# Four-layer graph network on one core: layer 1's aggregations run over four PSUM banks, and the out-attention's steps stand at other places

## The reference, cut to what matters

```python
def _gat_heads(x, adj, W, a):
    Wh = einsum('bnf,hfo->bhno', x, W)
    f1 = einsum('bhno,ho->bhn', Wh, a[:, :O])
    f2 = einsum('bhno,ho->bhn', Wh, a[:, O:])
    e = f1[:, :, :, None] + f2[:, :, None, :]
    e = where(e > 0, e, 0.01 * e)
    e = where(adj[None, None] > 0, e, -1e9)
    return einsum('bhnm,bhmo->bhno', softmax(e, axis=-1), Wh)
h = elu(_gat_heads(x, adj, W_heads, a_heads))
h = transpose(h, (0, 2, 1, 3)).reshape(B, N, -1)
out = elu(_gat_heads(h, adj, W_out[None], a_out[None])[:, 0])
y = maximum(out @ w1 + b1, 0) @ w2 + b2 + out
```

## Time and profile before

| | |
|---|---|
| timed runs | median 3086.3 us of 3 (3083.88 to 3086.51) |
| profiled execution | 3088.17 us, its span 3086.5 us |
| layer 0 | to about 417 us of the span |
| layer 1, the loop over pairs | first `project` at 425.8 us, last `out_part` before 2156 us |
| PE busy | 3025.1 us (98% of the span) |
| DVE, POOL, ACT busy | 75%, 69%, 56% |

### The profile page before, as it was taken

One profiled execution on the slowest core, in us unless ns is written; L12 is line 12 of the kernel. 1 busy time (PEld: TensorE's weight loads), 2 busy tenths in 40 slices (PEclk: granted clock), 3 DMA queues, 4 the chain that ended last, 5 costly groups with the idle time before them and its releaser, 6 DMA issues.

```text
span 3086.5 us, 65234 instructions
## 1 busy us (share of the span) xinstructions
PE 3025.1 (98%) x19324; PEld 2655.5 (86%) x19324; DVE 2321.6 (75%) x4877; ACT 1726.6 (56%) x4250; POOL 2120.1 (69%) x2901
## 2 busy tenths in 40 slices
PE   8999989999999999999999999999799999999997
PEld 7888878888998988888889888898688888888885
DVE  7777646777777777777777777675788888888885
ACT  3333335555555555555555555553577677776675
POOL 5666645666676666667666666651588888888885
PEclk9999989999999999999999999999999999999999
DMA  5555421112111111211111111112623333233220
GB/s 201 181 187 177 154 83 32 52 44 54 38 54 48 51 51 44 54 38 54 48 48 54 44 50 42 54 45 71 189 90 102 93 101 94 89 99 102 92 75 32
DMA packets 308643, 247.65 MB, mean 80 GB/s; under 512 B 150060, under 2 KB 215644, under 8 KB 308316
## 3 DMA queue, kind: packets, MB, share of 16 engines
q1 hardware_dynamic: 296796, 221.64, 24.1%
q10 hardware_dynamic: 9216, 16.78, 1.4%
q0 software_dynamic: 2560, 8.39, 0.8%
HBM read 162.83 MB, written 83.91 MB: 80 GB/s over the span
## 4 chain that ended last, share of the span: by engine, by line
PE 79%; issue 3%; POOL 3%; DVE 1%; DMA 0%; ACT 0%; SPq 0%; POOLq 0%; DVEq 0%; ACTq 0%
PE hp L2048 24%; PE wop L2062 23%; PE wop L47 9%; PE hp L2188 5%; PE hp L47 5%; PE agg L2031 5%; PE shared L2070 2%; PE shared L2155 2%; PE agg L2155 2%; PE shared L262 1%; POOL g_terms L1361 1%; POOL cols L403 0%; PE smallp L212 0%; PE smallp L101 0%; POOL x1b L1374 0%
## 5 line engine op out<-in xcount | busy, mean ns | idle before, releaser
L1293 POOL TENSOR_TENSOR w_first<-xd,v_row 128x512 f32<-128x512 f32 x480 | 690.9, 1452 | 351.1 <-DMA xd<-x_scratch 275.8
L2048 PE MATMUL hp<-yT_hi,big_hi 128*128 128x256 f32 x2048 | 583.7, 285 | 1.4 <-DVE yT_lo L1737 1.4
L2048 PE MATMUL hp<-yT_hi,big_lo 128*128 128x256 f32 x2048 | 580.7, 284 | 0.0
L2048 PE MATMUL hp<-yT_lo,big_hi 128*128 128x256 f32 x2048 | 580.4, 283 | 0.0
L2062 PE MATMUL wop<-big_hi,hT_hi 128*128 128x512 f32 x1024 | 424.7, 415 | 0.0
L1754 DVE TENSOR_TENSOR hT_lo<-ex,hT_hi 128x512 fp32r<-128x512 f32 x256 | 258.6, 1010 | 200.9 <-ACT hT_hi L1452 198.3
L2062 PE MATMUL wop<-big_hi,hT_lo 128*128 128x512 f32 x1024 | 401.5, 392 | 0.0
L2062 PE MATMUL wop<-big_lo,hT_hi 128*128 128x512 f32 x1024 | 400.0, 391 | 0.0
L2048 PEld LDWEIGHTS hp<-yT_hi,big_hi 128*128 128x128 f32 x2048 | 393.5, 192 | 6.8 <-DVE yT_lo L1737 1.7
L2048 PEld LDWEIGHTS hp<-yT_lo,big_hi 128*128 128x128 f32 x2048 | 393.6, 192 | 1.2
L2048 PEld LDWEIGHTS hp<-yT_hi,big_lo 128*128 128x128 f32 x2048 | 393.6, 192 | 0.0
(11 more groups left out here) (215 smaller groups left out, 8009.2 us busy)
## 6 DMA issues: line engine op xcount, KB each, us to landing
x0f<-in_x_turned SPq DMA_DIRECT2D x64, 256.0 KB, 2.7
xt<-in_x SPq DMA_DIRECT2D x64, 256.0 KB, 3.0
x_scratch<-w_first ACTq DMA_DIRECT2D x64, 256.0 KB, 2.3
xa<-x_scratch SPq DMA_DIRECT2D x64, 256.0 KB, 2.7
att_hi_scratch<-att_hi SPq DMA_DIRECT2D x64, 256.0 KB, 2.0
att_lo_scratch<-who SPq DMA_DIRECT2D x64, 256.0 KB, 2.0
att_hi<-att_hi_scratch SPq DMA_DIRECT2D x64, 256.0 KB, 3.6
att_lo<-att_lo_scratch SPq DMA_DIRECT2D x64, 256.0 KB, 4.3
```

The costliest lines, as they stand in the source:

```text
L1293: nc.gpsimd.tensor_tensor(terms[:, k % TR, :], xd[:], v_row[:, k, :], ALU.mult).then_inc(terms_ready, 1)
L2048: ins = nc.tensor.matmul(hp[half][:, s * 2 * P:(s + 1) * 2 * P], a, b, start=c == 0 and i == 0, stop=c == KC - 1 and i == 2)
```

## The change

It turns `smallp` and `shared` into one tensor `agg_b` of two banks that is the second target of `aggregate`. Tile 0 of a pair goes to `agg`, tile 1 to `agg_b`, in one call for both. The four halves are carried off in the order of `EVICTED`. What uses `smallp` and `shared` in between stands behind `banks_free`, which waits until all four are off. `at.dve_before_exp` is split in two calls for every second tile. The lists of all five engines are written anew; DVE's, ACT's and POOL's instructions are the same in number and shape.

```diff
     def dve_before_exp(self, nc, dve, t, p, j, fill):
+        self.dve_add(nc, dve, t, p, j)
+        self.dve_peak(nc, dve, t, fill)
...
-            smallp = pb("smallp", [P, D])
-            shared = pb("shared", [P, D])
+            agg_b = pb("agg_b", [P, 2, D])
+            shared, smallp = agg_b[:, 0, :], agg_b[:, 1, :]
+            banks = (agg, agg_b)
+            EVICTED = ((0, 0), (1, 0), (0, 1), (1, 1))
...
-                def y_hi(p, q, j, side):
+                def y_hi(p, q, n):
+                    j, side = EVICTED[n]
                     act.wait_ge(agg_done, 4 * p + 2 * q + j + 1)
                     ge(act, h_done, 2 * (4 * p + 2 * q + side - 1))
-                    ge(act, y_lo_ready, 2 * (4 * p + 2 * q + j) + side)
+                    if n > 1:
+                        act.wait_ge(y_lo_ready, 4 * (2 * p + q) + n - 1)
...
-                def aggregate(p, q, j):
+                def aggregate(p, q, before):
+                    a = 2 * p + q
+                    for j in range(2):
+                        pe.wait_ge(at.turned_ready, 2 * (2 * p + j + 1))
+                        pe.wait_ge(xa_loaded[j], 16 * p + 16)
+                        ge(pe, y_lo_ready, 4 * a - 1 + j)
+                        if j == 1:
+                            before()
+                        for c in range(KC):
+                            for g in range(2):
+                                own = slice(g * NODES, (g + 1) * NODES)
+                                ins = nc.tensor.matmul(by_head(banks[j][:, g, :])[:, :, c, :],
+                                                       xa[j][own, c * P:(c + 1) * P],
+                                                       at.turned[own, j, 2 * q:2 * q + 2, :], start=True, stop=True)
+                        ins.then_inc(agg_done, 1)
+                def banks_free(p, q):
+                    pe.wait_ge(y_lo_ready, 4 * (2 * p + q) + 4)
```

More of the change, by code:

```diff
@@ L1335, in step @@
                     if fresh(p + 2):
[L1336 to L1342, removed]
+                        products_of(*second, range(0, 2))
                     if pair(m):
@@ L1494, in step @@
-                    if pair(p + 1):
-                        if later(p):
-                            dots(*d1, (2,))
+                    if fresh(p + 2):
+                        dots(*first, (0,))
                     if pair(p - 2):
                         split_att(2 * (p - 2) + 1, 1, p - 1)
[L1499 to L1504, removed]
+                    exp(k, 1)
@@ L1521, in step @@
+                    for n in range(3):
+                        y_hi(p, 1, n)
+                    if pair(p + 1):
+                        at.act_exp(nc, act, 2 * p + 3)
+                    y_hi(p, 1, 3)
+                    h_hi(k + 1, 0)
+                    if fresh(p + 2):
+                        dots(*first, (5, 6))
+                    h_hi(k + 1, 1)
                     if pair(p + 1):
                         at.act_turned(nc, act, 2 * p + 2, p + 1, 0, agg_done)
-                    if pair(p):
-                        exp(k + 1, 1)
@@ L1829, in step @@
                     if pair(m):
                         ao_.dve_after_exp(nc, dve, 2 * m)
-                    if pair(p + 1):
-                        at.dve_before_exp(nc, dve, 2 * p + 3, p + 1, 1, fill1)
-                    if pair(p):
-                        elu(k + 2, 0)
+                    for n in range(4):
+                        y_lo(p, 1, n)
+                    h_lo(k + 1, 0)
+                    if pair(m):
+                        out_f(2 * m + 1, 1)
                     if pair(p + 1):
@@ L1855, in step @@
-                    if pair(p):
-                        elu(k + 3, 1)
-                    if pair(p + 1):
-                        y_lo(p + 1, 0, 1, 0)
-                    if pair(p):
-                        h_lo(k + 3, 0)
-                    if pair(p + 1):
-                        y_lo(p + 1, 0, 1, 1)
-                for j in range(2):
-                    for side in range(2):
-                        y_lo(0, 0, j, side)
+                        for n in range(4):
+                            y_lo(p + 1, 0, n)
@@ L1867, in _ @@
+                    h_lo(k + 3, 0)
+                for n in range(4):
+                    y_lo(0, 0, n)
                 dve.wait_ge(a_loaded, 16)
@@ L2118, in step @@
                         ao_.pe_scores(nc, pe, 2 * m + 1, same_graph)
-                    if pair(p):
-                        out_part(p, 1, 3)
-                    if pair(m):
-                        pe.wait_ge(at.turned_ready, capped(2 * (2 * p + 4), 2 * T))
-                        out_sums(2 * m, 0)
-                    if pair(p + 1):
-                        aggregate(p + 1, 0, 0)
-                    if pair(p):
-                        project(p, 3)
+                    for c in range(KC):
+                        out_part(p, 1, c)
```

343 lines of the change are left out of this document (141 added, 202 removed).

## The result

The changed kernel is slower: median 3174.26 us of 4 runs (3173.82 to 3176.88), against 3085.89 us of 4 runs of the kernel before. The ratio is 1.0289, interval 1.0271 to 1.0307. The prediction said 3075.0 with a range of 3053 to 3100, so the result lies outside it, on the side of the rivals. The profiled execution took 3176.88 us, its span 3175.2 us.

What follows compares the result with a forecast made beforehand. It took TensorE's blocks to bound the kernel at 54.17 us a step; -1.02 saved, +0.8 wait and -0.1 gaps gave 53.85, in all -11.3 us, so 3075.0 us, range 3053 to 3100.

Steps and rivals of the forecast that it cites:

- What bounds the kernel: Layer 1 steps: TensorE's blocks alone set the step, 54.17 us, apart from short issue gaps of 0.34 us.
- first rival: TensorE in layer 1's steps: no wait at all, 3051 us; chance 20%.
- Part 2: Small transpositions and scores on TensorE: placing them side by side saves about 0.08 per pairing, 0.24 us a step.
- Part 1: TensorE's aggregations: two runs of 32 passes replace four of 16, saving 0.39 us twice, 0.78 a step.
- the gaps called issue: TensorE's short gaps, mostly ahead of transpositions: 0.34 us a step, expected to shrink by 0.1.
- Part 3: TensorE at banks_free(p, 1), ahead of at's transposition: a new wait of 0.8 us a step for the last y_lo.
- the other new waits come out with room: TensorE's waits at both transpositions of ao, banks_free(p + 1, 0) and att_ready: room of 0.8 to 2 us, no cost.
- the second one: VectorE held up behind GpSimd's products, making the banks_free wait 1.5 us a step: 3096 us; chance 20%.
- The third: A second new wait behind out_part(p, 1), for ao's probabilities and att_ready: 3105 us; chance 8%.
- That the run saves nothing: Aggregation over four banks: nothing saved, 0.78 us a step dearer, 3100 us; chance 7%.
- The prediction's own sign of being wrong: TensorE's waits fall on another block, or the part outside layer 1 changes by more than 2 us.
- the case without a wait: TensorE in layer 1's steps never waits at the new places: 3051 us; chance 20%.

Runs made afterwards that it cites:

- e9: Changed kernel with ao's add first, two out_part chunks ahead of the run, who's copy earlier, product 5 later, dot 5 behind an exp: 3051.75 us.
- e10: As e9, but the two out_part chunks stand between the tiles of aggregate(p, 1), splitting one run: 3063.82 us.
- e7: Changed kernel with GpSimd's product 5 of the first tile moved behind the out-attention's probabilities: 3118.21 us.
- e2: Changed kernel with two of the four chunks of out_part(p, 0) moved ahead of aggregate(p, 1), the run left whole: 3093.04 us.
- e8: Changed kernel with three moves: ao's add first, two out_part chunks ahead of the run, who's copy ahead of dots 1 and 2: 3081.16 us.
- e1: Changed kernel with the first operation (add) of the out-attention's softmax moved ahead of at.dve_peak in VectorE's list: 3089.41 us.
- e6: Changed kernel with two out_part chunks placed between the tiles of aggregate(p, 1), so that run is split in two: 3095.18 us.
- e4: Changed kernel with the copy of who, keep_wo(m, 0), moved ahead of dots 1 and 2 in ScalarE's list: 3157.31 us.

## Why the prediction was wrong

**What bounds the kernel** was right for the kernel before, and the sum of TensorE's blocks was priced well: without a wait the prediction gave 3051 for its first rival, and e9 has 3051.75. That it is so near is luck in part, since two of its terms were off in opposite ways (Part 2).

**Part 1** held. One run of 32 passes is 1.98 us. e10 shows that it saves 0.34 us beside a score, and the blocks put it at 0.40 without one; I had taken 0.39.

**Part 2** was wrong where it was tried. The transposition costs 0.11 at either place, so its switch to float32 and back was never the price I had made of it. The pairing of the score with out_sums was not tried alone, but the chain of e9 shows the same 0.17 with and without it. So the 0.24 a step was nothing. In its place came two gains that I had put lower or not at all. A step was 54.17 in the mean and 53.96 without the gaps called issue, so these gave 0.21 and not 0.1; and an out_part in one piece takes 5.47 us where two halves took 2.75 each, 0.03 for each of the three that are no longer cut.

**Part 3** is where it failed. The two times that it counted came out: `who` was put at T + 13.2 and came at T + 13.4 (out_f starts at 13.7), the last `y_lo` at T + 25.8 and came at T + 26.0. The second is luck in part: `h_lo` and the first elu together took 1.4 us more than their terms, held up by GpSimd, and `at.dve_peak` with ao's own operations 1.2 us less. But both times were held against one wait alone, `banks_free(p, 1)`. The step "the other new waits come out with room" listed four others and left out the one inside the run, `scores_read`, although the diff shows it as an argument of `aggregate`; so this wait stood in the sum at nothing, with no reason given. The prediction's own terms give it a price: 13.2 + 2.3 for out_f and natural + 0.98 for h_lo + 1.3 for the one elu that stands there + 2.45 for `at.dve_peak` + 0.2 for L109 itself put the end of the read at T + 20.4; TensorE, with 5.75 + 5.5 + 0.24 + 5.75 + 0.17 + 1.09, is there at T + 18.5. That is a wait of about 2.0, and behind it `banks_free` costs nothing. The step would have been 54.17 - 1.02 + 2.0 - 0.1 = 55.05, and the forecast, with the prediction's other small terms, near 3111: slower, which is the right way, and still too low. The measured wait is 2.93, which by the same sum gives 3139; it is longer because `who` and out_f came 0.45 later and `h_lo` and the elu took 1.4 more, less what the rest of the way took less.

The 24 falls of the clock, 38 us more, were in no part of the prediction. In the trace of before TensorE never waited for more than 0.7 us from step 1 to step 31, and it shows no fall there, so the price could not be read from it; but the sum had no term and no bound for it either. 3139 and these 38 make 3177, against 3174.26 measured.

**The rivals.** Two of them were half right. VectorE is held up behind GpSimd, as the second one said: `ex` at 1.49 in place of 0.42 and `hT_lo` at 1.50; e7 shows that product 5 alone is worth 56 us, by way of the wait and of the falls. But I let it act on `banks_free`, where it made 3096. The third saw a second wait, at the wrong place; e2 and e8 show the places where the next ones stand, once the first is gone. That the run saves nothing fell with e10. The prediction's own sign of being wrong, waits of TensorE on another block, is what came. Its range did not fit its chances: the case without a wait had 20% and stood at 3051, below the lower end of 3053.

**What stays open.** The way through the other engines of e1, e2 and e6 (54.5 us a step) was not taken apart operation by operation; that it is there follows from e2 and e6 having one step for two amounts of TensorE's work. How product 5 and dot 5 share the 29.4 us between e8 and e9 is open too.

## What to carry to other kernels

When two uses are put into one buffer, list every wait that the shared buffer brings, those inside a helper too, and hold each against the time at which the queue of the engine that releases it gets there: here a sum that was already made for one wait would have shown the other, and the right direction with it. In a list that an engine works off in order, let the small operation that frees a resource go ahead of the long group that only shares its engine; here one 0.22 us add behind one group made most of 88 us. A wait of TensorE may cost more than its own length, since the passes behind it can run at half clock, so a wait of two or three microseconds in a loop is to be priced with the passes behind it.

## What the runs showed of the hardware

The granted clock fell to 0.50 behind waits far shorter than a step, in a kernel that keeps TensorE busy for 96% of the span, and not each time: with a wait of 2.93 us in 24 of 28 steps, with 2.65 in 18, with 1.9 in 6, and with 1.2 or less in none. Each fall made the step 1.6 us longer. Eleven passes of no use in the place of the wait took all of the falls away and 28.6 us off the time.

Some operations of VectorE that start inside one of GpSimd's are held until that one is done: 1.49 in place of 0.41, and 1.66 in place of 0.69. It is not all of them. In the profile of after, from 500 to 2100 us, all 140 `h_lo` that start inside a GpSimd operation of over 0.5 us, with 0.2 us of it left, end 0.54 to 0.55 us behind it, and all 112 such first operations of an elu 0.28 to 0.29 us behind it. The second operation of an elu and `y_lo`, which read PSUM, take 0.69 inside as outside, and a reduction over SBUF (L238) takes 0.42 inside as outside. Of two moves meant to bring VectorE to its read earlier, the one that makes it start out_f earlier, inside a product (e4), gained 0.3 us of wait, and the one that takes the product away (e7) 1.0.
